# A Perceiver layer on one core: squares turned two steps ahead, an output stage in PSUM, another order of the expert weights

## The reference

```python
def xattn(x):                    # cross attention
    h, c = lin(x, hW, hb), lin(ctx, cW, cb)
    q, k, v = lin(h, qW, qb), lin(c, kW, kb), lin(c, vW, vb)
    return lin(softmax(q @ k.T / sqrt(512)) @ v + q, oW, ob)
def ssm(x):                      # a long convolution, by Fourier transforms
    xp, z = split((layernorm(x) * ln_g + ln_b) @ in_w.T + in_b)
    y = irfft(rfft(xp) * rfft(kernel(A_log, B_param, C_param, log_dt)))
    return clip((y * silu(z)) @ out_w.T + out_b + x, -10, 10)
def ffn(x):                      # each token goes to its best expert of eight
    e = argmax(softmax(x @ gate_w + gate_b))
    return x @ expert_w[e] + expert_b[e]
x = x + xattn(layernorm(x)); x = x + ssm(layernorm(x)); x = x + ffn(layernorm(x))
```

## Time and profile before

| | us |
|---|---|
| median of 3 runs | 1179.87 |
| lowest, highest | 1178.14, 1180.66 |
| profiled execution, own time | 1175.85 |
| span of its instructions | 1174.1 |

### The profile page before, as it was taken

The page is one execution under the profiler, slowest core; times in us unless marked ns, Lnnn a source line. Parts: engine busy times, 40 slices in busy tenths (PEclk is TensorE's granted clock), DMA queues, the critical chain, the costliest instruction groups (busy, mean ns, idle before and its releaser), DMA issues.

```text
span 1174.1 us, 16673 instructions
## 1 busy us (share of the span) xinstructions
PE 1100.5 (94%) x4945; PEld 884.9 (75%) x4945; DVE 942.4 (80%) x1943; ACT 508.5 (43%) x1091; POOL 490.9 (42%) x432
## 2 busy tenths in 40 slices
PE   7999999999999999999989999999999999974497
PEld 5787877788887888878767877877878888862365
DVE  7953588988898899865398999999999765897684
ACT  4221165555555555443544444444444353322362
POOL 4702253454444444312244543444445235183543
PEclk9999999999999999999999999999999999996599
DMA  8311488887787776323366866776685610025892
GB/s 282 101 53 36 78 204 204 211 199 197 172 194 186 187 190 173 125 81 72 67 189 180 189 186 172 189 184 173 182 199 161 202 37 8 30 73 179 306 347 81
DMA packets 202198, 184.36 MB, mean 157 GB/s; under 512 B 18160, under 2 KB 147216, under 8 KB 202146
## 3 DMA queue, kind: packets, MB, share of 16 engines
q1 hardware_dynamic: 180930, 141.26, 47.5%
q10 hardware_dynamic: 17856, 32.51, 7.8%
q0 software_dynamic: 3360, 9.97, 2.3%
HBM read 142.77 MB, written 42.73 MB: 158 GB/s over the span
## 4 chain that ended last, share of the span: by engine, by line
PE 44%; DVE 20%; issue 13%; DMA 10%; POOL 7%; SPq 3%; ACT 1%; DVEq 0%; POOLq 0%; ACTq 0%
PE bank L557 22%; PE bank L696 10%; DMA xb<-in_ctx_dram 5%; PE bank L745 3%; PE bank L923 3%; DVE h L1472 2%; DVE mx L1530 2%; DMA p_rows<-probs 2%; POOL hl_A L1912 2%; DVE rows L1576 2%; POOL hl_B L1919 2%; POOL hl_C L1919 2%; POOL hl_F L1912 2%; PE bank L780 1%; DVE xb L1559 1%
## 5 line engine op out<-in xcount | busy, mean ns | idle before, releaser
L1068 ACT ACTIVATE probs<-bank,nbias 128x512 f32<-128x512 f32 x128 | 88.1, 688 | 305.5 <-DVE nbias L1535 305.5
L696 PE MATMUL bank<-hl_A,probsT 128*128 128x512 f32 x768 | 191.6, 398 | 4.2 <-DVE probsT L1547 3.8
L696 PE MATMUL bank<-hl_F,probsT 128*128 128x512 f32 x768 | 190.8, 397 | 3.2 <-POOL hl_F L1912 1.8
L557 PE MATMUL bank<-hl_C,hl_D 128*128 128x512 f32 x768 | 186.4, 391 | 6.3 <-ACT probs L1068 6.1
L557 PE MATMUL bank<-hl_B,hl_D 128*128 128x512 f32 x768 | 185.3, 391 | 1.4 <-POOL hl_B L1919 1.1
L696 PEld LDWEIGHTS bank<-hl_A,probsT 128*128 128x128 f32 x768 | 143.5, 188 | 41.8 <-DVE probsT L1547 6.4
L557 PEld LDWEIGHTS bank<-hl_C,hl_D 128*128 128x128 f32 x768 | 143.5, 188 | 41.1 <-ACT probs L1068 7.4
L696 PEld LDWEIGHTS bank<-hl_F,probsT 128*128 128x128 f32 x768 | 144.0, 188 | 38.6 <-POOL hl_F L1912 2.2
L557 PEld LDWEIGHTS bank<-hl_B,hl_D 128*128 128x128 f32 x768 | 143.6, 188 | 34.9 <-issue 2.3
L1912 POOL TENSOR_TENSOR hl_A<-stage,hl_A 128x512 fp32r<-128x512 f32 x64 | 84.5, 1321 | 201.2 <-ACT hl_A L1035 201.2
L1912 POOL TENSOR_TENSOR hl_F<-stage,hl_F 128x512 fp32r<-128x512 f32 x64 | 85.8, 1340 | 187.0 <-ACT hl_F L1035 187.0
(11 more groups left out here) (416 smaller groups left out, 1913.9 us busy)
## 6 DMA issues: line engine op xcount, KB each, us to landing
p_rows<-probs ACTq DMA_DIRECT2D x124, 256.0 KB, 3.0
stage<-in_ctx_dram SPq DMA_DIRECT2D x112, 256.0 KB, 3.4
spectra<-in_ctx_dram SPq DMA_DIRECT2D x64, 256.0 KB, 6.2
xb<-in_ctx_dram SPq DMA_DIRECT2D x64, 256.0 KB, 5.6
resid<-p_rows SPq DMA_DIRECT2D x248, 64.0 KB, 2.1
stage<-in_L_ffn_expert_w_dram SPq DMA_DIRECT2D x9, 1024.0 KB, 7.1
h<-p_rows SPq DMA_DIRECT2D x124, 64.0 KB, 2.6
obB<-p_rows SPq DMA_DIRECT2D x124, 64.0 KB, 2.0
```

The costliest lines, as they stand in the source:

```text
L557: last = nc.tensor.matmul(dst, lhs[:, a, t, k * P:(k + 1) * P], rhs[:, c, t, :], start=(t == 0 and (a, c) == PASSES[0]), stop=(t == T - 1 ...
L696: last = nc.tensor.matmul(obank[u % 2][:], probsT[u % 2][:, a, j, :], nat[b][par][:, c, j, :], start=(j == 0 and (a, c) == PASSES[0]), sto ...
L1068: nc.scalar.activation(dst, src, ACT.Exp, bias=nbias[:, q:q + 1], scale=SCALE, accum_out=rsum[:, q:q + 1]).then_inc(probs_ready, 1)
```

## The change

1. `next_square` takes how far ahead it works. Before the loop three blocks of chunk 1 are turned as before; in the first trip step 0 turns the fourth, step 1 none, and from step 2 on each step turns the block two steps on. The first block of a new chunk is so turned in steps 2 and 6.
2. The inputs of batch 1 get their bias in PSUM; ScalarE rounds from there, and VectorE makes each remainder from there one tile behind the addition. `stage[0]` is no longer used for it, so table 0 can be loaded after `outT.3`.
3. The first four products of each half wait for the second copied spectrum, not the fourth.
4. The output stage of both batches works in the bank: residual added, clipped, then added to x. Two tiles of batch 0 stand before the gating of batch 1, two behind it.
5. GpSimd prepares the residual of batch 1 first, without waiting for VectorE's products, and that of batch 0 behind it.
6. `EARLY` is 2: GpSimd makes the remainders of tables 0 and 1, VectorE those from table 2 on. The raw buffers go round in fours; tables 2 and 3 are loaded earlier; VectorE makes the remainders of tables 2 and 3 behind the turned tokens 0 and 1, and in step g those of table g+4 (before: g+6).
7. The split of the experts' biases stands before `gate`. The logits of batch 1 are copied to `obB`. ScalarE rounds table 5 behind the tokens of tiles 0 and 1.

The diff at its core; new and removed semaphores, names, and waits that only follow from them are left out:

```diff
@@ -28,15 +28,14 @@
 GROUPS = E + SPARE
 SLOTS = 6
-EARLY = 3
-RAW = (0, 1, 0, 1, 0, 2, 3, 1, 0, 2, 3, 1, 0, 2, 3)
+EARLY = 2
+RAW = (0, 1, 0, 1, 2, 3, 0, 1, 2, 3, 0, 1, 2, 3, 0)
 ROWS_KEPT = 8
...
 BLOCKS_OF_STEP = ((0, 1), (2,), (3,), ())
 FIRST_BLOCKS = ((0, 1, 2), (3,), (), ())
-TURNED_AHEAD = 3
 LAG = 4
@@ -98,6 +97,9 @@
 COPIED = {name: k + 1 for k, name in enumerate(n for n in JOBS if kind(n) in COPIED_KINDS)}
 EVACUATED = [n for n in JOBS if kind(n) not in COPIED_KINDS]
+for _k in (2, 3):
+    EVACUATED.remove(f"x_ssm.{_k}@0")
+    EVACUATED.insert(EVACUATED.index("x_ssm.0@1"), f"x_ssm.{_k}@0")
 EVAC = {name: k + 1 for k, name in enumerate(EVACUATED)}
@@ -450,7 +451,7 @@
                 if last is None:
                     if n == 0:
-                        sp.wait_ge(u_lo[1], T)
+                        sp.wait_ge(filled, JOB["outT.3"] + 1)
                     elif n == 1:
@@ -519,13 +520,14 @@
                 sp.dma_start(probs[0][half * E:half * E + E, :], expert_b).then_inc(in_eb, 16)
             fixed_load(1)
+            fixed_load(2)
             for b in range(B):
-                sp.wait_ge(x_ready[b], T)
+                evacuated_by(sp, f"x_ssm.3@{b}")
                 sp.dma_start(mixed_tiles[b][:, :, D:2 * D], xb[:, b]).then_inc(x_stored, 16)
+            fixed_load(3)
             for b in range(B):
                 store_rows(b)
-            for g in (2, 3, 4):
-                fixed_load(g)
+            fixed_load(4)
             for g in (5, 6, 7):
@@ -1135,8 +1142,12 @@
             def round_inputs(b):
                 for k in range(T):
-                    act.wait_ge(evacuated, EVAC[f"u.{k}@{b}"])
-                    nc.scalar.activation(u_hl[b][:, 0, k, :], u_rows[b][:, k, :], ACT.Copy).then_inc(u_hi[b], 1)
+                    if b == 0:
+                        act.wait_ge(evacuated, EVAC[f"u.{k}@0"])
+                    else:
+                        act.wait_ge(u_biased, k + 1)
+                    nc.scalar.activation(u_hl[b][:, 0, k, :], uT[:, k, :] if b == 0 else bank_of(f"u.{k}@1")[:], ACT.Copy
+                                         ).then_inc(u_hi[b], 1)
@@ -1211,9 +1222,9 @@
                 weights(3)
                 weights(4)
-                weights(5)
                 turned_tokens(0)
                 turned_tokens(1)
+                weights(5)
                 for g in range(GROUPS):
@@ -1551,9 +1562,9 @@
                     nc.vector.transpose(tbank[u % 2][:], moved[b][u % 2]).then_inc(p_moved, 1)
-                def next_square(t, u):
-
-                    par, dd = ((u + TURNED_AHEAD) // T + 1) % 2, (u + TURNED_AHEAD) % T
+                def next_square(t, u, ahead):
+
+                    par, dd = ((u + ahead) // T + 1) % 2, (u + ahead) % T
                     if dd == 0:
@@ -1597,8 +1608,11 @@
                         if not (first and u < 2):
                             row_sums(*back(t, u, 2))
-                        if not (last and u + TURNED_AHEAD >= T):
-                            next_square(t, u)
+                        if first and u < 2:
+                            if u == 0:
+                                next_square(t, u, T - 1)
+                        elif not (last and u + 2 >= T):
+                            next_square(t, u, 2)
                         if not kernel_terms and u % 3 != 2 and u < 7:
@@ -1641,12 +1655,24 @@
                 return last
-            def inputs(b):
-                if b == 1:
-                    dve.wait_ge(in_ub, 16)
-                for k in range(T):
-                    filled_by(dve, f"u.{k}@{b}")
-                    nc.vector.tensor_tensor(u_rows[b][:, k, :], bank_of(f"u.{k}@{b}")[:], ubB[:], ALU.add).then_inc(evacuated, 1)
+            def inputs():
+
+                for k in range(T):
+                    filled_by(dve, f"u.{k}@0")
+                    nc.vector.tensor_tensor(uT[:, k, :], bank_of(f"u.{k}@0")[:], ubB[:], ALU.add).then_inc(evacuated, 1)
+
+            def inputs_in_place():
+
+                dve.wait_ge(in_ub, 16)
+                for k in range(T + 1):
+                    if k < T:
+                        dst = bank_of(f"u.{k}@1")
+                        filled_by(dve, f"u.{k}@1")
+                        nc.vector.tensor_tensor(dst[:], dst[:], ubB[:], ALU.add).then_inc(u_biased, 1)
+                    if k > 0:
+                        dve.wait_ge(u_hi[1], k)
+                        nc.vector.tensor_tensor(u_hl[1][:, 1, k - 1, :], bank_of(f"u.{k - 1}@1")[:],
+                                                u_hl[1][:, 0, k - 1, :].bitcast(F32), ALU.subtract).then_inc(evacuated, 1)
@@ -1697,20 +1725,16 @@
                     gated_lo(T - 1)
-            def take_output(b, k):
-
-                r = resid[b][:, k, :]
+            def add_output(b, k):
+
+                name = f"x_ssm.{k}@{b}"
+                y = bank_of(name)
                 dve.wait_ge(resid_ready[b], k + 1)
-                filled_by(dve, f"x_ssm.{k}@{b}")
-                nc.vector.tensor_tensor(r, bank_of(f"x_ssm.{k}@{b}")[:], r, ALU.add).then_inc(evacuated, 1)
-
-            def add_output(b, k):
-
-                r = resid[b][:, k, :]
-                dve.wait_ge(evacuated, EVAC[f"x_ssm.{k}@{b}"])
-                link(nc.vector.tensor_scalar(r, r, 10.0, -10.0, ALU.min, ALU.max))
-                nc.vector.tensor_tensor(xb[:, b, k, :], xb[:, b, k, :], r, ALU.add).then_inc(x_ready[b], 1)
-                dve.wait_ge(x_ready[b], k + 1)
+                filled_by(dve, name)
+                link(nc.vector.tensor_tensor(y[:], y[:], resid[b][:, k, :], ALU.add))
+                link(nc.vector.tensor_scalar(y[:], y[:], 10.0, -10.0, ALU.min, ALU.max))
+                nc.vector.tensor_tensor(xb[:, b, k, :], y[:], xb[:, b, k, :], ALU.add).then_inc(evacuated, 1)
+                dve.wait_ge(evacuated, EVAC[name])
                 return row_statistics(xb[:, b], k)
@@ -1844,44 +1868,37 @@
                 gate_output(0)
                 lo_rows("normT.#@1", hlA)
-                inputs(1)
-                for k in range(T):
-                    dve.wait_ge(u_hi[1], k + 1)
-                    nc.vector.tensor_tensor(u_hl[1][:, 1, k, :], u_rows[1][:, k, :], u_hl[1][:, 0, k, :].bitcast(F32),
-                                            ALU.subtract).then_inc(u_lo[1], 1)
+                inputs_in_place()
                 outputs(0)
...
                 outputs(1)
                 outputs_lo(1)
-                for k in range(T):
-                    take_output(0, k)
+                for k in range(2):
+                    add_output(0, k)
                 gate_output(1)
-                for k in range(T):
+                for k in range(2, T):
                     last = add_output(0, k)
...
                 output_means(0)
                 for k in range(T):
-                    take_output(1, k)
                     last = add_output(1, k)
...
                 for b in range(B):
                     lo_rows(f"ffnT.#@{b}", ffn_hl[b])
+                split_expert_bias()
                 gate()
                 route()
-                split_expert_bias()
-                weight_los(3)
-                weight_los(4)
-                turned_lo(0)
-                turned_lo(1)
-                weight_los(5)
+                for g in range(2):
+                    turned_lo(g)
+                    weight_los(g + 2)
                 for g in range(GROUPS):
...
                     if g + 2 < GROUPS:
                         turned_lo(g + 2)
-                    if g + SLOTS < GROUPS:
-                        weight_los(g + SLOTS)
+                    if g + 4 < GROUPS:
+                        weight_los(g + 4)
@@ -2030,11 +2047,12 @@
                 if b == 0:
-                    pool.wait_ge(in_outb, 16)
                     pool.wait_ge(x_back[0], 16 * T)
                     filled_by(pool, "normT.3@1")
                 else:
-                    pool.wait_ge(product_step, PRODUCTS * (TRIPS + 2))
+                    pool.wait_ge(in_outb, 16)
+                    pool.wait_ge(rows_ready, ROWS["norm@1"] + 1)
+                    pool.wait_ge(gated_lo_done[0], T)
                 for t in range(T):
@@ -2091,8 +2109,8 @@
                 outputs_lo()
                 gated_lo()
+                residual(1)
                 residual(0)
-                residual(1)
                 routing_tables()
```

20 lines of the change are left out of this document (13 added, 7 removed).

## The result

The changed kernel takes 1191.76 us (median of 4 runs, 1189.74 to 1194.71); the one before, beside it on the same chip, 1179.2. The ratio is 1.0106, 95% interval 1.0079 to 1.0132: slower by 12.6 us, where +5.0 was forecast. The profiled execution took 1190.5 us, its span is 14.7 longer.

The account below looks back on a forecast made before the run. It took VectorE to bound the second attention loop, with TensorE's floor just above VectorE's shortened trip. Terms -7.5 - 0.5 - 0.4 + 1.3 - 5.0 + 17.1 = +5.0 gave median 1184.9 us; own range 1179 to 1193, 8-in-10 range 1170 to 1197.

Parts of the forecast that it names:

- rival 3: Second attention loop gains nothing, VectorE's small products stretched by GpSimd elsewhere, trip near 46: +12.5, 1192 us; chance 0.13.
- the residuals: Tail: GpSimd's reordered residual additions run beside VectorE's products, each costing 1.1 us: +1.3, bounds 0 and +2.5.
- the expert term: Expert stage: remainders four tables ahead make loads late, so products end 91.2 us after gather_rows instead of 74.1: +17.1.
- the cycle: Expert stage: remainders, load, landing, rounding, tokens, next remainders in turn; 13.1 us each, three for tables 8, 10, 12.
- L = 6.5: Expert stage: time in us from a table load's issue to landing, taken between the least 5.4 and median 7.1.
- tokens 0: Expert stage: first tile's tokens ready on VectorE 8.2 us after gather_rows, 9.0 before, less the traffic.
- VectorE's trip becomes 46.0 - 1.8 = 44.2: Second attention loop: squares two steps ahead remove the waits on memory; trip taken as 44.6, term -7.5.
- The output stage: Tail: output stage in PSUM, clips at 0.70, takes 28.8 us against 33.8: -5.0, bounds -7 and 0.

Follow-up runs that it names:

- x2: The kernel before with only the new order of the expert weights; 1197.2 us.
- x3: The changed kernel with VectorE making remainders of tables 2 and 3 before the tokens, and in step g those of g+6, not g+4; 1169.7 us.
- x4: The kernel before with only the squares turned two steps ahead; 1173.8 us.
- x8: The kernel before with only the output stage in PSUM, two tiles of batch 0 ahead of the gating; 1175.8 us.
- x7: On x3, GpSimd makes the residual of batch 0 first and that of batch 1 behind VectorE's products, as before; 1166.3 us.
- x11: The kernel before with only the second loop's spectrum products moved right behind the maxima, squares still three ahead; 1168.0 us.
- x1: The changed kernel with only the order of the expert weights undone; 1172.5 us.

## Why the prediction was right and wrong

The measured 1191.8 is slower, as forecast, and inside the forecast's own range of 1179 to 1193, though 6.9 us above the forecast itself. It is also what rival 3 gave, 1192, and for rival 3's reason; that the sum fits so closely is partly luck, since the two profiles differ by 14.7, the expert stage cost 3.3 more and the residuals 1.3 more than taken, and the stretch before `gather_rows` gave 2.3 back.

**The direction and the expert term were right.** ScalarE waited for tables 6, 8, 10, 12 and 14, x2 and x3 show that the depth of the remainders does it, and the cycle was 12.8 us where 13.1 was worked out. The term was 20.4 instead of 17.1. The load of table 6 landed late, 9.3 us behind its request at 1099.33 where L = 6.5 was taken, with table 7's, asked for at 1102.34, and the gathers beside it: +2.7 with tokens 0. The four cycles gave -1.2. Behind the start of table 14's rounding it took 23.3 us instead of 21.5; 1.4 of these 1.8 lie in product 10, the first after a pause:

```profile
1163.40 4.47 PE L928 MATMUL bank<-hl_F,probsT 128*128 128x512 f32 x12 [2.36 <-DVE probsT L1855]
...
1168.64 3.05 PE L928 MATMUL bank<-hl_B,probsT 128*128 128x512 f32 x12
```

Its matrix products took 4.47 us for the 3.05 of the next one, at a mean granted clock of 0.65 from 1163.40 to 1167.87, and 1.00 behind. The sum took all of them at the quick rows.

**The step that failed is the loop's: "VectorE's trip becomes 46.0 - 1.8 = 44.2".** It took 1.78 us of waiting out of VectorE's trip and left the durations behind it as they were. They were what they were because VectorE had been waiting while GpSimd worked. The term measured -0.2 (-0.9 alone, in x4). It also counted five trips between two stores of the chain as all of them, where six lie between the first and the last, so by its own price it should have read -8.9. Rival 3 named this ("VectorE's small products are stretched by GpSimd elsewhere") and had 0.13; it was given too little. What spoke against it, that the first loop holds its floor with similar work, was a bad comparison: its term (L1584) is one operation a step and no group of small products, and VectorE has 5.1 us of rest in a trip there. One trip of the first loop before, by window:

```profile
300.00:344.30 44.30, 44.30 (x194) 36.05 (x193) 39.22 (x79) 24.95 (x56) 20.71 (x16) 1.00 0.79 188
```

The trace of before had the evidence for rival 3 as well: groups of four products that took 1.46 us in one step of the trip, and 3.06 and 4.25 in two others, for the same work. The first two of these:

```profile
757.99 3.06 DVE L1472 TENSOR_TENSOR h<-qc,spectra 128x128 f32 x4
758.14 1.45 POOL L1912 TENSOR_TENSOR hl_F<-stage,hl_F 128x512 fp32r<-128x512 f32 x1 [2.66 <-ACT hl_F L1035]
...
776.38 0.97 DVE L1472 TENSOR_TENSOR h<-h 128x128 f32<-128x128 f32 x2
777.28 0.49 DVE L1472 TENSOR_TENSOR h<-resid,spectra 128x128 f32 x2
```

Of the miss of 9.7 us in the span, 7.3 are the loop's.

The Trainium skill (SBUF — State Buffer, Who interferes with whom) says that a VectorE instruction with two SBUF inputs contends with a GpSimd one that reads SBUF, and that one with at most one such input, outside the modes that use both ports, does not. The traces agree: the products pay up to 1.1 us for each addition they meet, while the transposes of squares stay at 0.70 to 0.71 and the clips in PSUM at 0.70 beside the same additions. The clip in SBUF, with one input, did pay, 1.27 for 0.42; the exception for those modes would cover it, which no run here tests.

**The output stage was right to 0.1 us** (28.9 against 28.8; -4.9 alone in x8). **The residuals were mis-sized:** 2.6 us (x7) for the 1.3 taken, just above the bound of 2.5. The slack ahead of the rounding, 3.58 us in x7, hid what fell there, and was used up. Behind it stood two of GpSimd's additions, at 1.1 each (the rows of 2.39 and 1.77 above, 1.30 and 0.69 in x7), and a pair of products at 1017.25 that took 1.69 for 1.29 beside GpSimd's scaling of the residual, which the sum did not price. **Aggregation to `gather_rows`** had no term and gave 2.3. Before, GpSimd made the remainders of table 2 beside the small operations of the gate, shown first, and three of these took 2.7 us more than now, when it has done with its two tables:

```profile
1083.15 4.93 POOL L1903 TENSOR_TENSOR hl_E<-stage,hl_E 128x512 fp32r<-128x512 f32 x4 [18.94 <-ACT hl_E L1174]
1083.29 1.21 DVE L1757 TENSOR_TENSOR logit<-logit,desc 128x64 f32<-128x64 f32 x1
...
1085.75 1.20 DVE L1762 TENSOR_TENSOR ssm_in<-onehot,ssm_w 128x64 f32<-128x64 f32 x1
```
```profile
1079.65 0.22 DVE L1781 TENSOR_TENSOR logit<-logit,desc 128x64 f32<-128x64 f32 x1
...
1080.42 0.22 DVE L1786 TENSOR_TENSOR ssm_in<-onehot,ssm_w 128x64 f32<-128x64 f32 x1
```

The prediction counted table 2's move as traffic and as VectorE's work, not as GpSimd's work gone. The same contention is thus behind three of its errors: the loop, the residuals and the gate.

## What to carry over

When a wait on a busy engine is taken away, ask which engine worked meanwhile, and whether what follows the wait will now run beside it; an idle gap next to a shared resource can be worth nothing, and moving the sensitive operations into the other engine's rest, with the same work done, was worth 11.7 us of a loop here. When a buffer's release moves earlier or later in a list, count the cycle from release to next use in steps of the consumer, against what a load takes. In a list worked through in order, put what is due soonest first: one exchange of two lines took the pauses between the products from the expert stage.

## What the runs showed of the hardware

- A VectorE operation with both operands in SBUF that meets one of GpSimd's additions (1.2 to 1.5 us for 128 x 512) from its start pays 1.0 to 1.1 us, whatever its own size: 0.22 became 1.21 for 128 x 64, a pair of 128 x 128 went from 0.48 to 1.56, one of 128 x 512 from 0.68 to 1.77. The price is per meeting, not per element; a meeting with part of an addition cost less (1.02 for the pair in step 1 of the kernel before).
- The issue of the second gather took 5.75 to 5.76 us in the four kernels where the experts' biases are split behind `gather_rows` and VectorE's remainders of two tables begin 0.05 us after it (before, x4, x8, x11), and 1.20 where those remainders already ran (x1, x3), 0.94 or 0.95 where they came later (changed, x2). What it cost is not shown: TensorE's transposes of tile 1 and the first product wait for these rows, but they landed 12.2 us behind `gather_rows` before, with the long issue, and also in x1, with the short one. Why a later start of the remainders makes it pay their whole 4.9 us isn't settled.
- Landing times of 1 MB loads in one stage of the changed kernel: 9.3 us for each of two asked for 3.0 us apart, beside the gathers, and 5.4 for one asked for at 1115.47, when DMA traffic had been at rest.
- In the expert stage of the changed kernel the first product after TensorE had stood idle for 2.3 to 5.1 us took 4.42 to 4.52 us, at a mean granted clock of 0.64 to 0.65, which lies between the two levels of 1.2 and 2.4 GHz (0.5 and 1.00); the products between took 3.04 to 3.06, at 1.00.
